# Key heads computed inside the seven-product stages of the query heads

## The reference

```python
x = x + _L0_attn_ref(_L0_cond_ref(x, L0_cond_weights, itok_B_0_15), wq, wk, wv, wo)
x = x + _L0_ffn_ref(_L0_cond2_ref(x, itok_B_0_15, L0_cond2_weights), qweight, weight_scale, bias)

# _L0_attn_ref, B = T = 32, H = 32, KV = 8, HD = 128
q = (x @ wq).reshape(B, T, H, HD).transpose(0, 2, 1, 3)
k = (x @ wk).reshape(B, T, KV, HD).transpose(0, 2, 1, 3)
v = (x @ wv).reshape(B, T, KV, HD).transpose(0, 2, 1, 3)
q = q * cos + _rotate_half(q) * sin
k = k * cos + _rotate_half(k) * sin
k, v = jnp.repeat(k, 4, axis=1), jnp.repeat(v, 4, axis=1)
scores = einsum('bhtd,bhsd->bhts', q, k) / sqrt(HD)
att = softmax(where(tril, scores, -inf))
out = einsum('bhts,bhsd->bhtd', att, v)
return out.transpose(0, 2, 1, 3).reshape(B, T, H * HD) @ wo
```

## Time and profile before

| | us |
|---|---|
| median of 3 runs | 518.03 (518.0 to 518.05) |
| the profiled execution | 518.72 |
| its span | 516.8 |
| TensorE busy in the span | 504.7 |
| VectorE busy | 413.0 |
| GpSimd busy | 310.4 |
| ScalarE busy | 251.4 |

### The profile page before, as it was taken

How to read it: one execution, slowest core, us unless ns; L and a number is a source line. 1 busy time by engine, 2 the same in 40 slices (tenths; PEclk the granted TensorE clock), 3 DMA queues, 4 the chain that set the end, 5 groups by cost and what they waited for, 6 DMA issues and landing times.

```text
span 516.8 us, 9293 instructions
## 1 busy us (share of the span) xinstructions
PE 504.7 (98%) x3184; PEld 406.0 (79%) x3184; DVE 413.0 (80%) x648; ACT 251.4 (49%) x481; POOL 310.4 (60%) x308
## 2 busy tenths in 40 slices
PE   8999999999999999999999999999999999999994
PEld 6888888877888888888888888888888888778634
DVE  5459867899698969896888789877978788985696
ACT  2552644564446444644464537354735453423364
POOL 1658688988659756975697569747884653400000
PEclk9999999999999999999999999999999999999998
DMA  8345121320502050204020502050310006000004
GB/s 263 125 156 186 46 82 63 101 69 15 164 1 61 3 163 0 61 0 162 0 61 0 162 0 61 0 162 4 114 46 20 2 1 208 2 2 1 0 0 164
DMA packets 32645, 35.29 MB, mean 68 GB/s; under 512 B 2251, under 2 KB 22859, under 8 KB 32620
## 3 DMA queue, kind: packets, MB, share of 16 engines
q1 hardware_dynamic: 32620, 34.96, 21.0%
HBM read 28.66 MB, written 6.29 MB: 68 GB/s over the span
## 4 chain that ended last, share of the span: by engine, by line
PE 87%; DVE 6%; POOL 3%; issue 2%; DMA 1%; ACT 0%; SPq 0%; DVEq 0%; POOLq 0%; ACTq 0%
PE bank L743 23%; PE bank L744 22%; PE bank L745 22%; PE bank L813 3%; PE bank L802 3%; PE bank L715 3%; PE bank L717 3%; PE bank L716 3%; PE bank L686 1%; POOL q_rot L401 1%; PE bank L871 1%; POOL wq_lo L387 1%; PE bank L697 1%; DVE y L1319 1%; DVE xacc L1339 1%
## 5 line engine op out<-in xcount | busy, mean ns | idle before, releaser
L401 POOL TENSOR_TENSOR q_rot<-q_rot,q_swap 128x512 f32<-128x512 f32 x64 | 88.2, 1379 | 60.8 <-DVE q_swap L1096 60.8
L530 ACT ACTIVATE q_swap<-bank 64x512 f32<-64x512 f32 x80 | 47.7, 596 | 124.3 <-PE bank L745 76.9
L743 PE MATMUL bank<-wo_hi,o_hi 128*128 128x512 f32 x256 | 101.3, 396 | 0.8 <-issue 0.6
L744 PE MATMUL bank<-wo_lo,o_hi 128*128 128x512 f32 x256 | 99.8, 390 | 0.0
L745 PE MATMUL bank<-wo_hi,o_lo 128*128 128x512 f32 x256 | 99.7, 390 | 0.0
L1144 DVE TENSOR_TENSOR xacc<-xacc,bank 128x512 f32<-128x512 f32 x64 | 43.6, 681 | 37.1 <-PE bank L745 37.1
L1096 DVE TENSOR_TENSOR q_swap<-q_swap,cst 128x512 f32<-128x512 f32 x80 | 60.2, 753 | 0.0
L743 PEld LDWEIGHTS bank<-wo_hi,o_hi 128*128 128x128 f32 x256 | 48.0, 188 | 13.1 <-issue 2.6
L745 PEld LDWEIGHTS bank<-wo_hi,o_lo 128*128 128x128 f32 x256 | 48.1, 188 | 10.2
L744 PEld LDWEIGHTS bank<-wo_lo,o_hi 128*128 128x128 f32 x256 | 48.1, 188 | 9.5
L396 POOL TENSOR_TENSOR wo_lo<-raw_o,wo_hi 128x512 fp32r<-128x512 f32 x32 | 45.5, 1445 | 9.5 <-ACT wo_hi L516 9.5
(11 more groups left out here) (165 smaller groups left out, 1047.6 us busy)
## 6 DMA issues: line engine op xcount, KB each, us to landing
raw_q<-in_L_attn_wq SPq DMA_DIRECT2D x16, 512.0 KB, 4.0
raw_o<-in_L_attn_wo SPq DMA_DIRECT2D x8, 1024.0 KB, 7.0
v_st<-values SPq DMA_DIRECT2D x16, 256.0 KB, 4.4
xacc<-in_x SPq DMA_DIRECT2D x4, 512.0 KB, 7.2
raw_k<-in_L_attn_wk SPq DMA_DIRECT2D x8, 256.0 KB, 4.3
out<-xacc SPq DMA_DIRECT2D x8, 256.0 KB, 2.5
values<-v_more SPq DMA_DIRECT2D x6, 256.0 KB, 2.1
raw_o<-in_L_attn_wv SPq DMA_DIRECT2D x1, 1024.0 KB, 7.8
```

Source lines behind the costliest of these rows:

```text
L401: pool.tensor_tensor(item_out(h, k), item_out(h, k), q_swap[(h + k) % 2][:], ALU.add).then_inc(rope_done, 1)
L530: act.activation(dst[0:P // 2, :], ps[P // 2:P, :], ACT.Copy)
L743: pe.matmul(dst, l_hi, r_hi, start=(i == 0), stop=False)
L744: pe.matmul(dst, l_hi, r_lo, start=False, stop=False)
```

## The change

Two groups, 2p and 2p + 1, become five stages of seven block products; each stage makes two heads out of ten: (key 2p, query 0), (queries 1, 2), (query 3, key 2p + 1), (queries 0, 1) and (queries 2, 3) of the second group. The plain key products, wk_hi, wk_lo, raw_k and key_mm go. Items are four per stage. p runs over PAIRS = 4, with p = 1, 2 in the loop. There are three buffers raw_q in place of two and one raw_k, four for swapped halves (q_swap and v_more; others in the first pair), and the first product lies in the bank that was the key's. On GpSimd wo_low is split in two pairs around the weight sums; on ScalarE wo_high stays in two pairs. By V_BEFORE nine value tiles come before the first stage, and stages 0 to 3 of p = 0 take in 1, 1, 2 and 3 more. t_low(2) comes ahead of v_copy(8). The tail is as before.

```diff
-ITEMS = 1 + REP
+PAIRS = KV // 2
+STAGES = 5
+ITEMS = 4
-V_BEFORE = (9, 11, 15, 16)
+V_BEFORE = (9, 10, 11, 13, 16)
+V_SLOT = (0, 1, 2, 3, 4, 5, 0, 1, 2, 3, 4, 5, 2, 3, 2, 3)
...
+        def swap_of(p, i, k):
+            if k < 2:
+                return q_swap[k][:]
+            if isinstance(p, int) and p == 0 and i == 3:
+                return (v_slot[5], q_swap[1][:])[k - 2]
+            if isinstance(p, int) and p == 0 and i < 3:
+                return flat(s_nat[k - 2])
+            return v_more[k - 2][:]
...
         def _(pool):
+            def stage(p, i, split_wo=None):
+                more = not is_last(p, i)
                 if split_wo is not None:
                     wo_low(split_wo, 0, wo_lo)
                     wo_low(split_wo, 1, wo_lo)
+                if more:
+                    sum_weights(*following(p, i))
                 if split_wo is not None:
                     wo_low(split_wo, 2, wo_lo)
                     wo_low(split_wo, 3, wo_lo)
                 if more:
+                    for m in range(4):
+                        q_low(*following(p, i), m)
+                rope_add(p, i, 0)
+                rope_add(p, i, 1)
                 if more:
+                    q_low(*following(p, i), 4)
+                    q_low(*following(p, i), 5)
+                rope_add(p, i, 2)
+                rope_add(p, i, 3)
+                if more:
+                    q_low(*following(p, i), 6)
+            def stages(p):
+                stage(p, 0)
+                stage(p, 1)
+                stage(p, 2, split_wo=None if isinstance(p, int) and p == 0 else 2 * p - 1)
+                stage(p, 3)
+                stage(p, 4, split_wo=2 * p)
...
         def _(act):
+            def stage(p, i, last=None, soft=None, split_wo=None):
...
                 if more:
+                    for m in range(4):
+                        q_high(*following(p, i), m)
+                swap(p, i, 0)
+                swap(p, i, 1)
                 if more:
+                    q_high(*following(p, i), 4)
+                    q_high(*following(p, i), 5)
+                swap(p, i, 2)
+                swap(p, i, 3)
...
         def _(pe):
+                elif last is None:
+                    pe.wait_ge(rope_cos, ITEMS * n)
+                product(n, 1)
...
+            def scores(p, side, r):
                 if r == 0:
-                    pe.wait_ge(rope_done, 5 * (2 * g + 2))
+                    pe.wait_ge(rope_done, ITEMS * (STAGES * p + (3, 5)[side]))
+                    pe.wait_ge(first_kept, STAGES * p + (3, 5)[side])
...
+            def stage(p, i, last=None, fill=(), ahead=(), behind=(), end=(), side=None):
+                n = STAGES * p + i
+                for tile in ahead:
+                    project_out(*tile)
                 if last is not None:
+                    pe.wait_ge(rope_cos, ITEMS * n)
+                    if i in (0, 3):
+                        pe.wait_ge(s_turned, 4 * p + (0 if i == 0 else 2))
                     attend(*last)
+                products_of(p, i, last)
+                for tile in fill:
+                    values(tile)
+                for tile in behind:
+                    project_out(*tile)
+                if side is not None:
+                    scores(p, side, 0)
+                    scores(p, side, 1)
+                for tile in end:
+                    project_out(*tile)
+            def stages(p):
+                stage(p, 0, last=(2 * p - 2, 1), ahead=tiles(2 * p - 2, 0, 3), behind=tiles(2 * p - 2, 1, 0, 1))
+                stage(p, 1, behind=tiles(2 * p - 2, 1, 2, 3))
+                stage(p, 2, last=(2 * p - 1, 0), behind=tiles(2 * p - 1, 0, 0, 1, 2), side=0, end=tiles(2 * p - 1, 0, 3))
+                stage(p, 3, last=(2 * p - 1, 1), behind=tiles(2 * p - 1, 1, 0, 1, 2))
+                stage(p, 4, last=(2 * p, 0), ahead=tiles(2 * p - 1, 1, 3), behind=tiles(2 * p, 0, 0, 1, 2), side=1)
+            stage(0, 0, fill=late[0])
+            stage(0, 1, fill=late[1])
+            stage(0, 2, fill=late[2], side=0)
+            stage(0, 3, fill=late[3])
+            stage(0, 4, last=(0, 0), behind=tiles(0, 0, 0, 1, 2), side=1)
...
         def _(dve):
+                block_sum(p, i, 4)
+                rope(p, i, 0)
+                block_sum(p, i, 5)
+                rope(p, i, 1)
+                block_sum(p, i, 6)
+                rope(p, i, 2)
+                for tile in fill[0:1]:
+                    v_copy(tile)
+                for tile in behind[0:1]:
+                    accumulate(*tile)
+                rope(p, i, 3)
                 soft_part(5)
...
+            def stages(p):
+                stage(p, 0, last=(2 * p - 2, 1), weights=(2 * p - 1, 0), later=(), ahead=tiles(2 * p - 2, 0, 3),
+                      behind=tiles(2 * p - 2, 1, 0, 1))
+                stage(p, 1, weights=(2 * p - 1, 0), begin=(3, 4, 5, 6), later=(), behind=tiles(2 * p - 2, 1, 2, 3))
+                stage(p, 2, last=(2 * p - 1, 0), weights=(2 * p - 1, 1), behind=tiles(2 * p - 1, 0, 0, 1, 2), side=0,
+                      end=tiles(2 * p - 1, 0, 3))
+                stage(p, 3, last=(2 * p - 1, 1), weights=(2 * p, 0), behind=tiles(2 * p - 1, 1, 0, 1, 2))
+                stage(p, 4, last=(2 * p, 0), weights=(2 * p, 1), ahead=tiles(2 * p - 1, 1, 3), behind=tiles(2 * p, 0, 0, 1, 2),
+                      side=1)
```

More of the change, by code:

```diff
@@ L554, in _ @@
                 q_high(0, 0, i)
-            k_high(0)
             for i in range(4):
@@ L1144, in accumulate, with stage, soft_part @@
                 dve.tensor_tensor(xacc[:, tile, :], xacc[:, tile, :], w_ps[j % 2][:], ALU.add).then_inc(acc_done, 1)
-            def half(g, h, last=None, weights=None, fill=(), fill_last=(), soft_first=None):
-                def soft_part(*steps):
-                    if weights is not None:
-                        for step in steps:
+            def stage(p, i, last=None, weights=None, begin=(0, 1, 2), later=(3, 4, 5, 6), fill=(), ahead=(), behind=(), end=(), side=None):
+                def soft_part(*some):
+                    for step in some:
+                        if weights is not None and step in later:
                             soft(*weights, step)
-                def add_out(j):
-                    if last is not None:
-                        accumulate(*last, j)
-                soft_part(0, 1, 2)
-                rope(g, h, 0)
+                if weights is not None:
+                    for step in begin:
+                        soft(*weights, step)
+                for tile in ahead:
+                    accumulate(*tile)
                 if last is not None:
@@ L1202, in _ @@
-            half(1, 1, last=(0, 0), weights=(0, 1))
-            with dve.Fori(2, KV - 1) as g:
-                half(g, 0, last=(g - 2, 1), weights=(g - 1, 0))
-                half(g, 1, last=(g - 1, 0), weights=(g - 1, 1))
-            half(KV - 1, 0, last=(KV - 3, 1), weights=(KV - 2, 0))
-            half(KV - 1, 1, last=(KV - 2, 0), weights=(KV - 2, 1))
+                for tile in fill[2:]:
+                    v_copy(tile)
+                for tile in behind[2:]:
+                    accumulate(*tile)
@@ new lines, in stage, with tiles, stages @@
+                if side is not None:
+                    turn_scores(2 * p + side, 0)
+                    turn_scores(2 * p + side, 1)
+                for tile in end:
+                    accumulate(*tile)
+            def tiles(g, r, *which):
+                return [(g, r, j) for j in which]
+            def stages(p):
+                stage(p, 0, last=(2 * p - 2, 1), weights=(2 * p - 1, 0), later=(), ahead=tiles(2 * p - 2, 0, 3),
[6 more added lines that the diff above has]
+                      side=1)
@@ L1209, in round_w8 @@
+            dve.wait_ge(dma_const, 32)
+            stage(0, 0, fill=late[0])
+            stage(0, 1, fill=late[1])
+            stage(0, 2, fill=late[2], side=0)
+            stage(0, 3, weights=(0, 0), fill=late[3])
+            stage(0, 4, last=(0, 0), weights=(0, 1), behind=tiles(0, 0, 0, 1, 2), side=1)
+            with dve.Fori(1, PAIRS - 1) as p:
+                stages(p)
+            stages(PAIRS - 1)
             def round_w8(c):
```

482 lines of the change are left out of this document (205 added, 277 removed).

## The result

The changed kernel takes 546.81 us (median of 4 runs, 546.66 to 548.42) against 518.01 (4 runs) on the same chip: ratio 1.056, interval 1.0546 to 1.0571, slower by 28.8 us. 540 was predicted, with a range of 519 to 550. The profiled run took 548.42 us, its span 546.6, which is 29.8 more than before. One execution of four took far longer in experiment 4 (850.9 us) and in experiment 7 (999.7 us); these two slow ones are left out of the times given there.

The account below looks back on a forecast made before the run. TensorE, 98% busy, was taken to bound the kernel, with GpSimd's chains stalling it after the change. On 518.7 us: -5.4 - 0.4 + 17.7 + 10.4 = +22.3, so 541.0, taken as 540; own range 530 to 549, overall 519 to 550.

Parts of the forecast that it names:

- Stage 2's term: Loop, stage 2: scores wait for GpSimd's last rope addition, 24.0 us after stage start against TensorE's 18.98; stall 5.0 us.
- Stage 4's: Loop, stage 4: GpSimd's list ends at 20.2 us against TensorE's 18.98; stall 1.2 us.
- the second: GpSimd without pauses: each VectorE instruction with two SBUF inputs costs it some 0.44 us and itself waits.
- Loop and last pair: Stalls after the first pair: 3 x 5.1 + 2 x 1.2 = 17.7 us.
- The first pair: Stalls from late t_lo, late cosines, late scores and stage (0,4): together 10.4 us, ends 1.9 and 10.4.
- part (c): First pair, scores of stage (0,2): due 5.44 us after the last product, additions end at 9.8; stall 4.4 us.
- (b): First pair: GpSimd's backlog makes the last cosine late, 0.8 us in (0,1) and 1.8 in (0,2).
- (d): First pair, stage (0,4): GpSimd starts 1.1 us late with 7 exclusions, ends at 21.4; stall 2.4 us.
- Rival 3: TensorE's clock falls in holes of 3 to 5 us, 2 us each after six holes: 552 us; chance 0.04.
- Turns of 105.6: Sign that the forecast is right: two loop turns of about 105.6 us against 102.0 before.
- (1) free chains: GpSimd's pauses absorb exclusions and chains run nearly free: 520 us, about 529 with half the exclusions; chance 0.19.
- (2) faster: GpSimd keeps up and the 24 saved matmuls are won in full: 512 us; chance 0.12.

Follow-up runs that it names:

- experiment 4: Changed kernel with eleven purposeless 512-column matmuls put before the wait for the last rope addition in stages 2: 542.37 us, ratio 1.0479.
- experiment 7: Changed kernel with two buffers for swapped halves instead of four, each swap waiting for the addition two items back: 551.41 us, ratio 1.0588.
- Experiment 1: Changed kernel with GpSimd writing all seven low halves behind the four rope additions in stages 2 and 4: 529.07 us, ratio 1.0226.
- experiment 3: Changed kernel with VectorE's sine product replaced by an equal-size transpose with one SBUF input: 522.51 us, ratio 1.0085.
- experiment 8: Changed kernel with VectorE's accumulation handling 128 of 512 columns: 548.15 us, ratio 1.0572.
- experiment 2: Changed kernel with GpSimd's rope additions handling half of the columns: 519.45 us, ratio 1.0029.
- experiment 5: Experiment 1's order plus earlier swaps on ScalarE, output halves ahead of weight sums on GpSimd, softmax step 2 and accumulation moved on VectorE: 522.86 us, ratio 1.0094.
- experiments 6: Experiment 5's kernel with one value tile of the first pair moved from stage (0,3) to stage (0,0): 528.68 us, ratio 1.0199.
- experiment 9: Experiment 5's kernel with four more moves in VectorE's order, in stage 2 and the first pair: 526.15 us, ratio 1.0146.

## Why the prediction was right

**The chains (right, and shown).** Stage 2's term was 5.0 us; measured is 23.84 - 18.98 = 4.9. Stage 4's was 1.2; measured 20.48 - 18.98 = 1.5. Experiment 1 shows the first price (what GpSimd has ahead of the additions), experiment 3 the second (0.44 us per VectorE instruction with two SBUF inputs was forecast; without them two additions in stage 2 lose 1.00 and a low half 0.45), experiment 8 that VectorE's load isn't it. The 24 matmuls saved shorten a turn only in experiment 2, whose 101.47 is the single one below 102.0, and there half of each rope addition is left out.

**Loop and last pair.** 17.7 was forecast; the brackets from the turn on give 15.6, and the surcharges (six of 0.27, eight of 0.08 before scores and attends) 2.3, together 17.8. What I missed are 0.3 us per turn at the attend of stage 2, where I had the last cosine only 0.1 late.

**The first pair.** 10.4 was forecast. Brackets with surcharge: t_lo 0.5 (1.0), (0,1) 1.1 (0.8), (0,2) 2.9 (1.8), its scores 2.7 (4.4), stages (0,3) and (0,4) with the attend's wait for the softmax 2.5 (2.4): 9.7. The parts are off by up to 1.7; that the sum comes so near is luck, as their errors cancel. Why part (c) came out lower than forecast and (b) and (d) higher wasn't tested part by part.

**The clock (the missing term).** Rival 3 had a chance of 0.04 and belonged into the sum. I took "2 us each of six holes"; it fell at five: before the product at 77.05 (1.6 us), at the scores of 95.21, 198.50, 307.30 and 416.45 (3.46, 3.28, 3.48 and 3.52 instead of 1.95: 1.5, 1.3, 1.5, 1.6), 7.5 in all. Experiment 4 shows 1.3 of it by itself. My mistake was to let the forecast and rival 3 exclude one another: that the clock stays up behind stalls of some us rested on no row, since the trace before has no such hole.

**The sum.** -5.8 + 9.7 + 17.8 + 7.5 = +29.2, against 29.8 measured in the profiled runs; for the 0.6 left, short steps without a bracket are enough (0.4 in the turn from 138.17 on). Forecast was +22.3. The step that failed is thus the clock, which the sum put at nothing: 7.5 us, all that lies between forecast and measurement. The mechanism of the waits held.

**A slip in a check value.** "Turns of 105.6" doesn't follow from the terms: 102.0 - 1.4 + 5.1 + 1.2 = 106.9. The sum of the forecast didn't use it. Measured is 108.84: 106.9, 1.3 for the clock, 0.3 at the attend, 0.3 in stage 4.

**The rivals.** (1) free chains: against it stands 23.76 of 23.84 us; it would need pauses such as the order of experiment 1 makes. (2) faster: no order that I tried reaches it. The deciding point, stalls under 4.8 us in all, wasn't reached by experiment 5 with its 522.86. Whether an order exists that does is open: experiments 6 and 9 show that moves which close one hole open another, which isn't a proof that there is none.

**Not settled.** The split of the output weights wasn't undone by itself, only made one block again in experiment 5; DMA showed in none of the waits of TensorE.

## What to carry to other kernels

When matmuls are saved by giving more elementwise work to the other engines, an average load of 76% doesn't decide: follow the written order of each engine from one deadline of TensorE to the next, and place what the deadline asks for ahead of what merely prepares the next stage (17.7 us by one such move here, with the clock that it brought back). Count pairs of instructions that exclude one another as a cost of both engines, wherever one of them runs without pauses, and look again after each move, since the pause you use up was what kept the pair apart. A forecast hole of two to three microseconds on TensorE should carry the lowered clock behind it as a term of the sum: where the clock fell here it cost 1.3 to 1.8 us, and one hole of 2.66 us cost nothing.

## What the runs showed of the hardware

- The clock by holes, from brackets and the 64 scores behind them: after 1.98 us (experiment 3) 1.96 us, so still full; after 2.07 (experiment 9) 2.46; after 2.62 to 3.00 in the changed kernel 3.28 to 3.52. Where it fell, the slow stretch cost 1.3 to 1.8 us in all, the matmuls behind the scores included: in experiment 8 holes of 2.92 and 4.26 us were followed by scores of 2.97 and 2.78 and by a few slow matmuls, 1.6 us each time. The length of the hole alone doesn't tell whether it falls. The hole before product 1 of (0,2), all but equal in four kernels, had slow matmuls behind it at once after 2.65 (experiment 1) and 2.66 (experiment 4), from the sixth matmul on after 2.64 (the changed kernel), and none at all after 2.66 (experiment 8, granted clock 1.00 throughout). In experiment 7 a hole of 1.82 had slow matmuls behind it and one of 1.94 had none.
- A hole on TensorE costs 0.27 us more than its bracket before 512-column matmuls and 0.08 more before scores and attends. A wait under 0.16 us has no bracket, by the 0.39 us shown of a matmul and its step of 0.2267.
- A VectorE instruction with two SBUF inputs beside a GpSimd without pauses prolongs both: GpSimd's addition from 1.25 to 1.74 and 1.83 us, VectorE's two-input instruction from 0.70 to 1.15 and 1.78. PSUM-reading instructions of VectorE left GpSimd alone (two output halves in 2.56).
